# Layer 0's residual by a second, block-transposed load of x, and an SP queue that issues each transfer as soon as its buffer is free

## The chip, the core and the metric

The kernel runs on one core of one Trainium2 chip. The metric is device microseconds of one execution of the whole program. The core has TensorE (PE) for matmuls, VectorE (DVE), ScalarE (ACT), GpSimd (POOL) and SyncE (SP), which here only issues DMA transfers. Each engine runs its own list of instructions in order. They wait for each other through semaphores alone, written out by hand.

## The reference

The input x has 64 images of 256 x 256 pixels with 16 channels, in float32. Two layers follow each other, and each adds a convolution of the normalised input to the input:

```python
def _gn(v, G=8, eps=1e-5):      # mean and variance over height, width and the 2 channels of a group
    ...
    return ((g - m) / jnp.sqrt(s + eps)).reshape(v.shape)
kern = jnp.einsum('lj,lk,li->ijkl', u, w, v)          # 3 x 3 kernel, 16 channels to 16, of rank one per output channel
out  = lax.conv_general_dilated(inputs, kern, window_strides=(1, 1), padding='SAME', ...)
x = x + relu(conv(_gn(x)) + b)     # layer 0, with u, v, w, b of L0
x = x + relu(conv(_gn(x)) + b)     # layer 1, with those of L1
```

## The kernel before, in words

**Layout.** One image at a time stays in SBUF. A DMA brings rows of x into `raw` (two rows of the image to a partition, `a` being the row of the two), and DVE transposes 32 x 32 blocks into `evens` (`N0`): a partition then holds a channel and a column parity within a quarter of the height, and the free dimension holds pairs of columns and 64 rows. Layer 0 writes its sum into `odds` (`T1`, two buffers, by image): there a quadrant of 32 partitions holds a quarter of the width, with all 256 rows, and the pairs of columns are shifted by one column. Layer 1 reads `odds` and ends in `result` (`T2`), which DVE transposes into `pixels` for the store.

**Rounds.** Each layer of each image has four rounds (`f` = 0 to 3) of 8 column pairs. A round of a layer is, on PE, 6 taps of the convolution (6 x 16 matmuls of 32 x 32 weights over 512 columns) into `ps_y`, and 2 more such groups (32 matmuls, with the constant 0/1 weights `perm`) into `ps_x`: these move the layer's input, the residual, into the layout of the output. ACT makes relu(`ps_y` + bias) into `R` (`relu`, L454 for layer 0 and L457 for layer 1), and DVE adds `ps_x` and `R` (`add`, L574 and L571). `ps_y` and `ps_x` fill the whole of PSUM, so there is one of each: the convolution of the next round waits for `relued`, the next residual product for `added`.

**Order.** The program's loop over `p` runs layer 0 of image `p` (4 rounds), then layer 1 of image `p - 1` (4 rounds). In layer 0, DVE follows each add by `turn_in` of image `p + 1` (L554). In layer 1 it follows each add by `turn_out` (L586). The sums for the normalisations are built beside this: of squares by ACT (L430), of `evens` by POOL (`folds`, L280), of the layer 0 result by the accumulator of the relu (`partial_relu`) plus the sum of x (L605, L606). Small matmuls (`group_sums` L299, `bias_product` L309) stand in the middle of certain rounds, after their third tap (`HOOK_AFTER`); they write into `ps_x` and wait there for `added`, and the following residual product waits for `mini_read`, i.e. until DVE has read their result (L612, L635). `wrap_pair` (L319) adds 16 small matmuls to round 0 of layer 0.

**Transfers.** All are issued by SP into one queue: per image 8 loads of `raw` (L186) and 8 stores of `pixels` (L196), 448 to 576 KB each. The function `pass_on` paces them: a load waits for the residual product of the round before (`x_filled`), a store for the convolution of the round (`y_filled`), so that one is issued about every half round.

Of the kernel before, what the change touches and what calls it, by code (L numbers as in the profile page):

```python
# [7 lines left out]
IMAGES, H, W, C = 64, 256, 256, 16  # L8
P = 128
Q = 32  # L10
# [24 lines left out]
TURNS = HALVES * ROUNDS + 4  # L35
HALO0, HALO1 = 2 * (QUADS - 1), QUADS
ODDS_SUM, ODDS_PAD = 1, 2
EVENS_SUM = 2
HOOK_AFTER = 2

# [38 lines left out]

def norms_before(y, p):  # L80
    return 2 * p + y


def squares_at(kind, p):

    if kind == "odds":
        return ROUNDS * (2 * p + 2) + (ROUNDS - 1 if p + 1 < IMAGES else 0)
    return ROUNDS * (2 * p + 1)


def build(nc, x, params, consts, out):
# [7 lines left out]

    with ExitStack() as ctx:  # L100
        def sb(name, shape):
            return ctx.enter_context(nc.sbuf_tensor(name, shape, fp32))
# [8 lines left out]
        pixels = sb("pixels", [P, HALVES, ROW])  # L111
# [13 lines left out]
        acc_relu = sb("partial_relu", [P, ROUNDS])  # L125
        sums = [sb(f"sums{y}", [P, 2]) for y in range(2)]
        mom = [sb(f"moments{y}", [P, 2]) for y in range(2)]
        center = [mom[y][:, 0:1] for y in range(2)]
# [3 lines left out]
        bias = sb("bias", [P, 2])  # L132
# [35 lines left out]
        turned_out = sem("turned_out")  # L168

# [3 lines left out]
        def _(sp):  # L173
# [15 lines left out]
            def store(p, f, a):  # L189
# [3 lines left out]
                if ROUNDS * p + f:  # L193
# [3 lines left out]
                             pixels[:, a, :].rearrange("p (q y) -> p q y", q=QUADS)[:, :, part]  # L197
                             ).then_inc(image_out[a], 16)

            def pass_on(n, loaded, stored):  # L200
                if n:
                    sp.wait_ge(x_filled, n)
                load(*loaded)
                sp.wait_ge(y_filled, n + 1)
                store(*stored)

            for p in range(2):
                for f in range(ROUNDS):
                    for a in range(HALVES):
                        if p == 0 or f < ROUNDS - 1 or a == 0:  # L210
                            load(p, f, a)
            for p in range(IMAGES + 1):
                if p < IMAGES:
                    pass_on(round_of(0, p, 0), (p + 1, 3, 1), (p - 2, 1, 1))
                    pass_on(round_of(0, p, 1), (p + 2, 0, 0), (p - 2, 2, 0))
                    pass_on(round_of(0, p, 2), (p + 2, 0, 1), (p - 2, 2, 1))
                    pass_on(round_of(0, p, 3), (p + 2, 1, 0), (p - 2, 3, 0))
                else:
                    store(p - 2, 1, 1)
                    store(p - 2, 2, 0)  # L220
                    store(p - 2, 2, 1)
                    store(p - 2, 3, 0)
                if p:
                    pass_on(round_of(1, p - 1, 0), (p + 2, 1, 1), (p - 2, 3, 1))
                    pass_on(round_of(1, p - 1, 1), (p + 2, 2, 0), (p - 1, 0, 0))
                    pass_on(round_of(1, p - 1, 2), (p + 2, 2, 1), (p - 1, 0, 1))
                    pass_on(round_of(1, p - 1, 3), (p + 2, 3, 0), (p - 1, 1, 0))
                else:
                    load(p + 2, 1, 1)
                    load(p + 2, 2, 0)  # L230
                    load(p + 2, 2, 1)
                    load(p + 2, 3, 0)
            store(IMAGES - 1, 1, 1)
            for f in (2, 3):
                for a in range(HALVES):
                    store(IMAGES - 1, f, a)
# [54 lines left out]
        def _(pe):  # L291
# [30 lines left out]
            def conv0(p, f):  # L322
                n = round_of(0, p, f)
                if n:
                    pe.wait_ge(relued, n)
                if f == 0:
                    pe.wait_ge(scaled0, p + 1)
                    pe.wait_ge(padded0, p + 1)
                    pe.wait_ge(halo0, HALO0 * (p + 1))
                for t in range(NTAP):  # L330
                    side, i = t // TAPS, t % TAPS
                    for q in range(QUADS):
                        for r in range(QUADS):
                            k = SLOTS * q + EACH * f + side
                            rows, part = slice(Q * r, Q * (r + 1)), slice(Q * q, Q * (q + 1))
                            done = nc.tensor.matmul(ps_y[part, r, :], w0[rows, t * Q:(t + 1) * Q],  # L336
# [9 lines left out]
                if n:  # L346
                    pe.wait_ge(added, n)
                if f == 0:
                    pe.wait_ge(mini_read, MINI["bias", 0, p] + 1)
                for side in range(SIDES):  # L350
                    for q in range(QUADS):
                        for r in range(QUADS):
                            k = SLOTS * q + EACH * f + side
                            done = nc.tensor.matmul(ps_x[Q * q:Q * (q + 1), r, :], perm[Q * r:Q * (r + 1), side, :],  # L354
                                                    N0[Q * r:Q * (r + 1), k:k + EACH, 1:1 + HQ],
                                                    start=(side == 0), stop=(side == SIDES - 1))
                done.then_inc(x_filled, 1)

            def conv1(p, f):
                n = round_of(1, p, f)  # L360
                t1 = T1[p % 2]
                pe.wait_ge(relued, n)
# [57 lines left out]
        def _(act):  # L420
# [11 lines left out]

            def stats_of_evens(p, f):
# [6 lines left out]
            def stats_of_odds(p, f):  # L440
                act.wait_ge(added, round_of(0, p, f) + 1)
                square(T1[p % 2][:, EACH * f:EACH * (f + 1), 1:1 + H],
                       junk[:].rearrange("p q x -> p (q x)")[:, 0:EACH * H].rearrange("p (k h) -> p k h", h=H),
                       acc[1][:, f:f + 1])

            def relu(y, p, f):
                n = round_of(y, p, f)
# [270 lines left out]
```

## Time and profile before

| | us |
|---|---|
| median of 3 runs | 4696.13 (4691.48 to 4697.93) |
| profiled execution | 4676.86 |
| its span in the trace | 4675.1 |
| PE busy | 4587.9 (98%) |
| DVE busy | 2845.1 (61%) |
| ACT busy | 2199.5 (47%) |
| POOL busy | 1265.0 (27%) |
| DMA queue of SP, share of 16 engines | 35.0% |

The granted TensorE clock is 0.997 of full speed over the span. The trace's PE records have ends that are modelled and overlap, so "98% busy" says that PE is hardly ever empty, not that no time is lost between rounds; the starts of the instructions tell more. The work repeats itself image by image: the layer 0 convolution of one image starts at 2331.06 us, and that of the image 31 later at 4559.63 us.

### The profile page before, as it was taken

The numbers are of one execution on the slowest core, as the hardware profiler recorded it, in microseconds if no ns is written. First come the engines' busy times: TensorE is split into PE (matmuls) and PEld (weight loads), VectorE is DVE, ScalarE is ACT, GpSimd is POOL, SyncE is SP. The second block draws the span as 40 slices with busy tenths as digits, with TensorE's granted clock in tenths as the row PEclk, the third lists the DMA queues.
The fourth block names the chain that finished last, engine by engine and source line by source line (L and its number), as shares of the span: only waits on it lengthen the run. The fifth ranks groups of instructions, "written<-read, shape, count | busy, mean of one in ns | idle before, by whom it ended". The sixth has DMA issues, their size and how long they took to land.

```text
span 4675.1 us, 288889 instructions
## 1 busy us (share of the span) xinstructions
PE 4587.9 (98%) x138240; PEld 2626.0 (56%) x138240; DVE 2845.1 (61%) x3341; ACT 2199.5 (47%) x2242; POOL 1265.0 (27%) x1093
## 2 busy tenths in 40 slices
PE   5999999999999999999999999999999999999999
PEld 3555555555555555555555555555555555555555
DVE  4656656566566566665666656656656666566564
ACT  4454444544445444444454444444544444445442
POOL 3322322323223222232232322322313223223230
PEclk9999999999999999999999999999999999999999
DMA  3333333333333333333333333333333333333323
GB/s 120 108 120 117 124 121 122 118 122 116 122 121 120 118 119 120 123 118 121 122 119 121 121 120 121 120 121 122 120 121 121 120 125 117 121 122 120 121 91 102
DMA packets 542278, 555.71 MB, mean 119 GB/s; under 512 B 16432, under 2 KB 541104, under 8 KB 541104
## 3 DMA queue, kind: packets, MB, share of 16 engines
q1 hardware_dynamic: 541104, 537.22, 35.0%
q8 instruction: 1083, 17.74, 1.6%
q14 instruction: 91, 0.75, 0.1%
HBM read 268.72 MB, written 268.44 MB: 115 GB/s over the span
## 4 chain that ended last, share of the span: by engine, by line
PE 94%; issue 3%; ACT 1%; DVE 0%; ACTq 0%; DVEq 0%
PE ps_y L374 35%; PE ps_y L336 34%; PE ps_x L399 12%; PE ps_x L354 10%; PE ps_y L319 2%; PE ps_x L299 1%; ACT relu L457 1%; ACT relu L454 0%; PE ps_x L309 0%; DVE evens L554 0%; DVE result L571 0%; ACTq L452 0%; DVE pixels L586 0%; DVEq L100 0%; ACT evens L465 0%
## 5 line engine op out<-in xcount | busy, mean ns | idle before, releaser
L374 PE MATMUL ps_y<-odds,scaled 32*32 32x512 f32 x49152 | 1766.8, 600 | 7.9 <-issue 2.2
L336 PE MATMUL ps_y<-evens,scaled 32*32 32x512 f32 x49152 | 1745.3, 598 | 23.6 <-ACT evens L465 8.3
L574 DVE TENSOR_TENSOR odds<-ps_x,relu 128x2048 f32<-128x2048 f32 x256 | 586.8, 2292 | 1110.7 <-PE ps_x L354 842.1
L374 PEld LDWEIGHTS ps_y<-odds,scaled 32*32 32x32 f32 x49152 | 808.0, 103 | 794.2 <-issue 376.4
L336 PEld LDWEIGHTS ps_y<-evens,scaled 32*32 32x32 f32 x49152 | 852.8, 103 | 699.8 <-issue 214.0
L457 ACT ACTIVATE relu<-ps_y,bias 128x2048 f32<-128x2048 f32 x256 | 503.8, 1968 | 1094.3 <-PE ps_y L374 942.7
L280 POOL TENSOR_TENSOR fold<-fold,evens 128x1024 f32<-128x1024 f32 x384 | 845.0, 2200 | 597.3 <-DVE evens L561 309.8
L571 DVE TENSOR_TENSOR result<-ps_x,relu 128x2048 f32<-128x2048 f32 x256 | 586.6, 2292 | 636.4 <-PE ps_x L399 439.2
L454 ACT ACTIVATE relu<-ps_y,bias 128x2048 f32<-128x2048 f32 x256 | 503.7, 1968 | 920.8 <-PE ps_y L336 910.6
L354 PE MATMUL ps_x<-evens,constants 32*32 32x512 f32 x16384 | 786.7, 596 | 0.0
L399 PE MATMUL ps_x<-odds,constants 32*32 32x512 f32 x16384 | 776.2, 604 | 0.0
L267 POOL COPY odds<-odds 32x256 f32<-32x256 f32 x256 | 102.0, 399 | 2078.3 <-DVE odds L574 2066.5
L554 DVE STREAM_TRANSPOSE evens<-raw 128x1024 f32<-128x1024 f32 (+2 forms) x512 | 621.6, 1260 | 5.2 <-DMA raw<-in_x 5.2
L430 ACT ACTIVATE junk<-odds 128x2048 f32<-128x2048 f32 x256 | 490.6, 1917 | 282.8 <-DVE odds L574 282.8
L586 DVE STREAM_TRANSPOSE pixels<-result 128x1024 f32<-128x1024 f32 x512 | 618.3, 1251 | 4.5
L354 PEld LDWEIGHTS ps_x<-evens,constants 32*32 32x32 f32 x16384 | 406.8, 103 | 161.7 <-issue 13.9
L399 PEld LDWEIGHTS ps_x<-odds,constants 32*32 32x32 f32 x16384 | 406.3, 103 | 155.9 <-issue 9.7
L430 ACT ACTIVATE junk<-evens 128x2048 f32<-128x2048 f32 (+2 forms) x256 | 487.7, 1905 | 7.3 <-DVE evens L561 4.5
L280 POOL TENSOR_TENSOR fold<-evens 128x1024 f32<-128x1024 f32 x64 | 153.2, 2394 | 603.4 <-DVE evens L554 603.4
L299 PE MATMUL ps_x<-sums,constants 32*32 32x2 f32 x4096 | 122.9, 173 | 45.0 <-DVE sums L602 39.1
L299 PEld LDWEIGHTS ps_x<-sums,constants 32*32 32x32 f32 x4096 | 100.5, 103 | 80.6 <-issue 38.5
L606 DVE TENSOR_TENSOR sums<-sums 128x1 f32<-128x1 f32 x64 | 134.3, 2099 | 2.2
(49 smaller groups left out, 1266.7 us busy)
## 6 DMA issues: line engine op xcount, KB each, us to landing
out<-pixels SPq DMA_DIRECT2D x512, 512.0 KB, 3.5
raw<-in_x SPq DMA_DIRECT2D x256, 512.0 KB, 3.9
raw<-in_x SPq DMA_DIRECT2D x128, 576.0 KB, 4.1
raw<-in_x SPq DMA_DIRECT2D x128, 448.0 KB, 3.5
parameters<-in_params SPq DMA_DIRECT2D x2, 96.5 KB, 2.0
constants<-in_consts SPq DMA_DIRECT2D x1, 81.0 KB, 2.0
```

What stands on the lines that cost most here:

```text
L280: nc.gpsimd.tensor_tensor(to, chunk(0) if d == 1 else to, chunk(d), ALU.add).then_inc(folded, 1)
L336: done = nc.tensor.matmul(ps_y[part, r, :], w0[rows, t * Q:(t + 1) * Q], N0[rows, k:k + EACH, i:i + HQ], start=(t == 0), stop=(t == NTAP - ...
L354: done = nc.tensor.matmul(ps_x[Q * q:Q * (q + 1), r, :], perm[Q * r:Q * (r + 1), side, :], N0[Q * r:Q * (r + 1), k:k + EACH, 1:1 + HQ], st ...
L374: done = nc.tensor.matmul(ps_y[Q * r:Q * (r + 1), q, :], w1[p % 2][Q * q:Q * (q + 1), t * Q:(t + 1) * Q], t1[Q * q:Q * (q + 1), k:k + EACH ...
L399: done = nc.tensor.matmul(ps_x[Q * r:Q * (r + 1), q, :], perm[Q * q:Q * (q + 1), side, :], t1[Q * q:Q * (q + 1), k:k + EACH, 1 + HQ * r:1 ...
L430: nc.scalar.activation(into, source, ACT.Square, accum_out=to).then_inc(squared, 1)
L454: ins = nc.scalar.activation(R[:], ps_y[:], ACT.Relu, bias=bias[:, 0:1], accum_out=acc_relu[:, f:f + 1])
L457: ins = nc.scalar.activation(R[:], ps_y[:], ACT.Relu, bias=bias[:, 1:2])
L554: nc.vector.transpose(turned[:, a, 1:1 + PAIRS, :].rearrange("p (q k) g -> p q k g", q=QUADS)[:, :, freed(f), :], pixels_in[:, :, freed(f) ...
L571: nc.vector.tensor_tensor(T2[:].rearrange("p q k h -> p q (k h)"), ps_x[:], R[:], ALU.add).then_inc(added, 1)
L574: nc.vector.tensor_tensor(T1[p % 2][:, EACH * f:EACH * (f + 1), 1:1 + H].rearrange("p k (r h) -> p r k h", h=HQ), ps_x[:].rearrange("p r ( ...
L586: nc.vector.transpose(to[:, :, EACH * f:EACH * (f + 1), :], result[:, a, :, :].rearrange("p (q k) g -> p q k g", q=QUADS)).then_inc(turned ...
```

## The change

What PE, ACT and DVE do for layer 0 is divided anew; layer 1 stays nearly as it was.

- PE: the residual product of layer 0 (32 matmuls a round, L354) is gone. The convolution's rounds use `ps_y` and `ps_x` in turn, and wait for the `added` of two rounds back. Round 1 waits for `mini_read` of the bias, since it writes `ps_x`.
- The residual comes from x by a second load. `load_rest` fetches, for each round, 1 MB in four DMAs of 32 partitions x 8 x 256 elements (for round 0, 240 elements, and four more DMAs of 32 x 8 x 16 for the column before) into `rest`, a ring of two rounds. DVE's `turn_rest` transposes it into `odds` in two halves of 128 x 1024 a round, spread by the tables `REST_IN_0` (within layer 0) and `REST_IN_1` (for the next image, within layer 1).
- `rectify_and_add` takes the place of ACT's relu and DVE's add in layer 0: four instructions of 128 x 512 a round compute max(`ps`, -bias) + `odds` in place. The result lacks the bias, a constant per channel, which is put back where `odds` is used: as a scalar in layer 1's `add`, and in the statistics (`center_odds`, and ACT's two passes over the round, `Square` and `Identity`, both with the bias, in place of relu plus one `Square`).
- SP: no `pass_on`. Loads, rest loads and stores stand in one fixed order, and each waits only for its buffer (and for the transfer before it of its own kind). `pixels` becomes a ring of two rounds of its own.

The diff, cut to what the prediction speaks of:

```diff
+RES_DMAS = (2 * QUADS, QUADS, QUADS, QUADS)
+REST_IN_0 = ((2, 1), (3, 0), (3, 1))
+REST_IN_1 = (((0, 0), (0, 1)), (), ((1, 0),), ((1, 1), (2, 0)))
@@ SP
+            def load_rest(p, f):
+                ...
+                    sp.wait_ge(rest_turned, HALVES * (ROUNDS * p + f - RING + 1))
+                size = EACH * Q
+                for q in range(QUADS):
+                    part, to = slice(Q * q, Q * (q + 1)), rest[Q * q:Q * (q + 1), f % RING, :, :]
+                    start = size * f - C
+                    if start >= 0:
+                        sp.dma_start(to, x_quarters[p, q][:, :, start:start + size]).then_inc(rest_in[f % RING], 16)
+                ...
-                    pass_on(round_of(0, p, 0), (p + 1, 3, 1), (p - 2, 1, 1))
-                    pass_on(round_of(0, p, 1), (p + 2, 0, 0), (p - 2, 2, 0))
+                    load(p + 1, 3, 1)
+                    load_rest(p, 3)
+                    store_both(p - 2, 3)
+                    load(p + 2, 0, 0)
+                    load_rest(p + 1, 0)
+                    load(p + 2, 0, 1)
+                    load(p + 2, 1, 0)
+                    load_rest(p + 1, 1)
+                ...
@@ PE conv0
-                if n:
-                    pe.wait_ge(relued, n)
+                ps = (ps_y, ps_x)[f % 2]
+                if f == 1:
+                    pe.wait_ge(mini_read, MINI["bias", 0, p] + 1)
+                if n > 1:
+                    pe.wait_ge(added, n - 1)
                 ...
-                for side in range(SIDES):
-                    for q in range(QUADS):
-                        for r in range(QUADS):
-                            k = SLOTS * q + EACH * f + side
-                            done = nc.tensor.matmul(ps_x[Q * q:Q * (q + 1), r, :], perm[Q * r:Q * (r + 1), side, :],
-                ...
@@ ACT
+                shifted(chunk, into, ACT.Square, bias[p % 2][:], acc[1][:, f:f + 1])
+                shifted(chunk, into, ACT.Identity, bias[p % 2][:], acc_odds[:, f:f + 1])
@@ DVE
+            def turn_rest(p, f, half):
+                ...
+                dve.wait_ge(rest_in[f % RING], 16 * rest_in_by(p, f))
+                if p > 1:
+                    dve.wait_ge(x_filled, relus_before(p - 2, f) + 1)
+                ...
+                nc.vector.transpose(T1[p % 2][:, k:k + each, 1:1 + H].rearrange("p k (j h) -> p j k h", h=Q),
+                                    source.rearrange("p j (k x) -> p j k x", x=Q)).then_inc(rest_turned, 1)
+            def rectify_and_add(p, f):
+                ...
+                dve.wait_ge(rest_turned, HALVES * (ROUNDS * p + f + 1))
+                ...
+                dve.wait_ge(y_filled, n + 1)
+                for r in range(QUADS):
+                    odds = T1[p % 2][:, EACH * f:EACH * (f + 1), 1 + HQ * r:1 + HQ * (r + 1)]
+                    done = nc.vector.scalar_tensor_tensor(odds, ps[:, r, :].rearrange("p (k h) -> p k h", h=HQ),
+                                                          floor[p % 2][:], odds, ALU.max, ALU.add)
+                done.then_inc(added, 1)
@@ DVE, main loop
-                        add(0, p, f)
+                        rectify_and_add(p, f)
+                        if f < ROUNDS - 1:
+                            turn_rest(p, *REST_IN_0[f])
                         if p + 1 < IMAGES:
                             turn_in(p + 1, f)
```

On PE, at layer 0 of one image in the middle of the program (rounds 1 to 3, then the start of layer 1), there stood:

```order
L336 MATMUL ps_y<-evens,scaled 32x512 x96
L354 MATMUL ps_x<-evens,constants 32x512 x32
L336 MATMUL ps_y<-evens,scaled 32x512 x96
L354 MATMUL ps_x<-evens,constants 32x512 x32
L336 MATMUL ps_y<-evens,scaled 32x512 x96
L354 MATMUL ps_x<-evens,constants 32x512 x32
L374 MATMUL ps_y<-odds,scaled 32x512 x48
L309 MATMUL ps_x<-moments,scaled 32x1 x4
```

and now, at the same place (L383 is layer 0's convolution, L412 layer 1's, L351 the bias product):

```order
L383 MATMUL ps_x<-evens,scaled 32x512 x96
L383 MATMUL ps_y<-evens,scaled 32x512 x96
L383 MATMUL ps_x<-evens,scaled 32x512 x96
L412 MATMUL ps_y<-odds,scaled 32x512 x48
L351 MATMUL ps_x<-center_odds,scaled 32x1 x4
```

The convolutions of layer 0 now follow each other directly, in the two halves of PSUM by turns.

On DVE, from the start of layer 0 of an image, there stood (L574 the add, L551 and L554 the transposes of the next image):

```order
L574 TENSOR_TENSOR odds<-ps_x,relu 128x4x8x64
L551 COPY ends<-raw 128x2x16
L554 STREAM_TRANSPOSE evens<-raw 128x4x7x32 x2
L574 TENSOR_TENSOR odds<-ps_x,relu 128x4x8x64
L554 STREAM_TRANSPOSE evens<-raw 128x4x8x32 x2
```

and now, from the last round of layer 1 on (L631 layer 1's add, L641 `turn_out`, L610 `turn_rest`, L695 and L696 the bias and its negative, L622 `rectify_and_add`, L591 `turn_in`):

```order
L631 SCALAR_TENSOR_TENSOR result<-ps_x,bias,relu 128x2048
L641 STREAM_TRANSPOSE pixels<-result 128x1024 x2
L610 STREAM_TRANSPOSE odds<-rest 128x8x4x32 x2
L695 TENSOR_TENSOR bias<-parameters,ps_x 128x1
L696 TENSOR_SCALAR floor<-bias 128x1
L622 SCALAR_TENSOR_TENSOR odds<-ps_y,floor,odds 128x8x64 x4
L610 STREAM_TRANSPOSE odds<-rest 128x8x4x32
L588 COPY ends<-raw 128x2x16
L591 STREAM_TRANSPOSE evens<-raw 128x4x7x32 x2
L622 SCALAR_TENSOR_TENSOR odds<-ps_x,floor,odds 128x8x64 x4
L610 STREAM_TRANSPOSE odds<-rest 128x8x4x32
L591 STREAM_TRANSPOSE evens<-raw 128x4x8x32 x2
```

Two rest transposes stand between the last `turn_out` and the reading of the bias, and one between `rectify_and_add` and `turn_in` in each of rounds 0 to 2; `rectify_and_add` is four instructions where the add was one.

## Rows read from the trace of the kernel before

**Rows 1.** The page's busy time: engine, busy us, share of span, instructions.

```profile
PE 4587.9 (98%) x138240; PEld 2626.0 (56%) x138240; DVE 2845.1 (61%) x3341; ACT 2199.5 (47%) x2242; POOL 1265.0 (27%) x1093
```

**Rows 2.** Chain that ended last, two rounds: start us, us, what.

```profile
2340.35 6.15 PE ps_y L336 x166
...
2346.93 2.11 PE ps_x L354 x57
2349.05 0.04 issue
2349.08 6.15 PE ps_y L336 x167
...
2357.81 6.15 PE ps_y L336 x166
...
2366.53 3.24 PE ps_y L374 x69
```

**Rows 3.** Timeline of such a round: start us, us, engine, line, [idle before <-releaser].

```profile
2346.97 1.97 ACT L454 ACTIVATE relu<-ps_y,bias 128x2048 f32<-128x2048 f32 x1 [2.25 <-PE ps_y L336]
2349.08 0.24 PEld L336 LDWEIGHTS ps_y<-evens,scaled 32*32 32x32 f32 x32 [0.94 <-ACT relu L454]
2357.88 2.29 DVE L574 TENSOR_TENSOR odds<-ps_x,relu 128x2048 f32<-128x2048 f32 x1 [4.06 <-PE ps_x L354]
2360.09 2.43 DVE L554 STREAM_TRANSPOSE evens<-raw 128x1024 f32<-128x1024 f32 x2
```

**Rows 4.** Timeline, PE at the first layer 0 matmuls of two images.

```profile
2331.06 1.16 PE L336 MATMUL ps_y<-evens,scaled 32*32 32x512 f32 x32
...
4559.63 0.70 PE L336 MATMUL ps_y<-evens,scaled 32*32 32x512 f32 x16
```

**Rows 5.** Groups by line and form: busy us, mean ns of one, idle before.

```profile
L574 DVE TENSOR_TENSOR odds<-ps_x,relu 128x2048 f32<-128x2048 f32 x256 | 586.8, 2292 | 1110.7 <-PE ps_x L354 842.1 <-ACT relu L454 268.6
L554 DVE STREAM_TRANSPOSE evens<-raw 128x1024 f32<-128x1024 f32 x256 | 311.6, 1263 | 3.2 <-DMA raw<-in_x 3.2
L554 DVE STREAM_TRANSPOSE evens<-raw 128x1152 f32<-128x1152 f32 x128 | 171.9, 1388 | 2.0 <-DMA raw<-in_x 2.0
L554 DVE STREAM_TRANSPOSE evens<-raw 128x896 f32<-128x896 f32 x128 | 138.1, 1126 | 0.0
L606 DVE TENSOR_TENSOR sums<-sums 128x1 f32<-128x1 f32 x64 | 134.3, 2099 | 2.2
L616 DVE TENSOR_SCALAR small<-moments,small 128x1 f32<-128x1 f32 x128 | 27.4, 214 | 4.6
L625 DVE TENSOR_SCALAR small<-small 128x1 f32<-128x1 f32 x128 | 19.7, 154 | 4.3
L280 POOL TENSOR_TENSOR fold<-fold,evens 128x1024 f32<-128x1024 f32 x384 | 845.0, 2200 | 597.3 <-DVE evens L561 309.8 <-DVE evens L554 250.8
L430 ACT ACTIVATE junk<-odds 128x2048 f32<-128x2048 f32 x256 | 490.6, 1917 | 282.8 <-DVE odds L574 282.8
L430 ACT ACTIVATION_READ_ACCUMULATOR junk<-odds 128x1 f32 x256 | 47.5, 186 | 0.0
```

**Rows 6.** Busy time in one image's stretch: PE, PEld, DVE, ACT, POOL, clock, DMA.

```profile
2300.00:2371.50 71.50, 71.31 (x2174) 40.70 (x2159) 44.26 (x51) 34.31 (x35) 19.78 (x17) 1.00 0.37 121
```

**Rows 7.** DMA queues: packets, MB, share of 16 engines; then issues to landing.

```profile
q1 hardware_dynamic: 541104, 537.22, 35.0%
q8 instruction: 1083, 17.74, 1.6%
...
out<-pixels SPq DMA_DIRECT2D x512, 512.0 KB, 3.5
raw<-in_x SPq DMA_DIRECT2D x256, 512.0 KB, 3.9
```

**Rows 8.** Timeline, PE's weight loads in layer 1 after a `group_sums`.

```profile
2318.06 0.72 PEld L374 LDWEIGHTS ps_y<-odds,scaled 32*32 32x32 f32 x33 [0.75 <-issue]
```

More of the change, by code:

```diff
@@ L77, with relus_before, rest_in_by @@
 MINI = small_products()
+def relus_before(p, f):
+    return ROUNDS * p + f
+def rest_in_by(p, f):
+    both = (RES_DMAS[f % RING], RES_DMAS[f % RING + RING])
+    return sum(both) * p + sum(both[:f // RING + 1])
 def norms_before(y, p):
@@ L131, in build @@
         edge = sb("edge", [P, 1])
-        bias = sb("bias", [P, 2])
+        bias = [sb(f"bias{i}", [P, 1]) for i in range(2)]
+        floor = [sb(f"floor{i}", [P, 1]) for i in range(2)]
+        bias1 = sb("bias_result", [P, 1])
         ps_y = ctx.enter_context(nc.psum_tensor("ps_y", [P, QUADS, BANK], fp32))
@@ L168, in build @@
         turned_out = sem("turned_out")
+        rest_in = [sem(f"rest_in{i}") for i in range(RING)]
+        rest_turned = sem("rest_turned")
         block = ctx.enter_context(nc.Block())
@@ L212, in _, with store_both @@
+            def store_both(p, f):
+                for a in range(HALVES):
+                    store(p, f, a)
+            for f in range(ROUNDS):
+                for a in range(HALVES):
+                    load(0, f, a)
+            load_rest(0, 0)
+            load_rest(0, 1)
+            for f in range(ROUNDS):
+                for a in range(HALVES):
+                    if f < ROUNDS - 1 or a == 0:
+                        load(1, f, a)
+            load_rest(0, 2)
             for p in range(IMAGES + 1):
@@ L223, in _ @@
[L223 to L232, printed above, removed]
@@ L237, in _ @@
+                n = round_of(1, p - 1, 0) if p else 0
+                load(p + 2, 1, 1)
+                for f in range(1, ROUNDS):
+                    load(p + 2, *((2, 0), (2, 1), (3, 0))[f - 1])
+                    if p:
+                        store_both(p - 1, f - 1)
+                    if f == 1:
+                        load_rest(p + 1, 2)
+            store_both(IMAGES - 1, 3)
             for a in range(HALVES):
@@ L335, in conv0 @@
                             rows, part = slice(Q * r, Q * (r + 1)), slice(Q * q, Q * (q + 1))
-                            done = nc.tensor.matmul(ps_y[part, r, :], w0[rows, t * Q:(t + 1) * Q],
+                            done = nc.tensor.matmul(ps[part, r, :], w0[rows, t * Q:(t + 1) * Q],
                                                     N0[rows, k:k + EACH, i:i + HQ], start=(t == 0),
@@ L431, in square, with shifted @@
                 squares[0] += 1
+            def shifted(source, into, function, by, to):
+                act.wait_ge(squared, squares[0])
+                nc.scalar.activation(into, source, function, bias=by, accum_out=to).then_inc(squared, 1)
+                squares[0] += 1
             def stats_of_evens(p, f):
@@ new lines, in rectify_and_add @@
+            def rectify_and_add(p, f):
+                n = round_of(0, p, f)
+                ps = (ps_y, ps_x)[f % 2]
+                dve.wait_ge(rest_turned, HALVES * (ROUNDS * p + f + 1))
+                if f == 0:
+                    dve.wait_ge(mini_read, MINI["bias", 0, p] + 1)
+                dve.wait_ge(y_filled, n + 1)
[4 more added lines that the diff above has]
+                done.then_inc(added, 1)
@@ L634, in take_bias @@
                 dve.wait_ge(mini_filled, MINI["bias", y, p] + 1)
[L635 to L636 removed]
+                given, product = par[y][:, PRM - 1:PRM], ps_x[:, 0, 0:1]
+                if y:
+                    nc.vector.tensor_tensor(bias1[:], given, product, ALU.subtract).then_inc(mini_read, 1)
+                else:
+                    step(nc.vector.tensor_tensor(bias[p % 2][:], given, product, ALU.subtract))
+                    nc.vector.tensor_scalar(floor[p % 2][:], bias[p % 2][:], -1.0, None, ALU.mult).then_inc(mini_read, 1)
             dve.wait_ge(const_in, 16 * 3)
@@ L645, in _ @@
             scale_weights(0, 0)
+            for f, half in ((0, 0), (0, 1), (1, 0), (1, 1), (2, 0)):
+                turn_rest(0, f, half)
             for p in range(IMAGES + 1):
```

143 lines of the change are left out of this document (65 added, 78 removed).

## The prediction

> **What bounds the kernel now.** I read the page's busy times first: PE is busy 98% of the span, DVE 61%, ACT 47% [rows 1]. The chain of waits then shows what a round of layer 0 consists of: the convolution starts at 2340.35, its results are complete at 2346.93, the residual product's last part takes 2.11 us more, and the next convolution starts at 2349.08, then at 2357.81 and, with layer 1, at 2366.53 [rows 2]. A round is thus 8.73 us. The timeline of the same round shows a second condition which falls at the same moment: ACT's relu starts at 2346.97 and takes 1.97 us, and PE's next weights have waited 0.94 us for it [rows 3]. So 2.15 us of each layer 0 round lie behind the convolution's end, covered by two things at once, the residual product and the relu that frees `ps_y`. To win them both must go, and the change does both: no product, and the other half of PSUM for the next round. DVE is not in this chain: it idles 1110.7 us before its adds [rows 5]. From the first layer 0 matmul of one image to that of the image 31 later are 4559.63 - 2331.06 = 2228.57 us [rows 4], 71.89 us an image; 64 of these are 4601 us, and the start and the end take the other 74.
>
> **What is removed on PE.** A round has 128 matmuls of one size; 96 stay. By count a round becomes 8.73 x 96/128 = 6.55 us; by the chain, 8.73 - 2.11 - 0.04 = 6.58. The true step may be a little under this, since the 8.73 still holds the idle turn to the next convolution. I take 6.5 (at least 6.4). Saved: 2.23 us a round, 8.9 an image with the same in round 0, whose small matmuls stay. Layer 1's rounds keep their chain: one `ps_y`, relu by ACT, product into `ps_x`.
>
> **DVE, the engine that gets the work.** Two neighbours in a row give what one instruction adds: the add starts at 2357.88 and lasts 2.29, and the transposes behind it start at 2360.09, so instructions overlap by 0.08 us [rows 3].
> - Rest transposes: 8 an image of 128 x 1024. The same form into `evens` takes 1.263 us [rows 5], 1.18 with the overlap: + 9.4 us an image. Source and target strides differ, which no row shows; between 1.1 and 1.6 us each, I take 1.26.
> - `rectify_and_add`: the add of 2048 elements takes 2.292 us. The transposes of 896 and 1152 elements take 1126 and 1388 ns, 1.02 ns an element [rows 5]; at that slope the add has 2.10 us for its elements and 0.19 once per instruction. A quarter of the elements gives 0.52 + 0.19 = 0.72 us. A scalar read from a tile costs more: 214 ns with two such against 154 with none [rows 5], 0.03 each. I take 0.75; the bounds are 0.57 (a quarter of 2.292, nothing once per instruction) and 2 x 0.72 (the two operations taken in turn). Four are 0.75 + 3 x 0.67 = 2.76 us for 2.29: + 0.5 a round, 1.9 an image.
> - Gone: L606, 2.1 us an image, and L605. L606 is one element per partition and takes 2099 ns, as much as POOL's fold of 2200 ns [rows 5]: with both its inputs in SBUF it waits until the fold is over. The new `center_odds` step is of that kind too; it stands where the folds should have ended, so I count 0.2 us, and know it can be 2.3.
>
> The Trainium skill (VectorE: DVE Perf Modes, The TRN2 errata) says that the fixed latency falls between instructions, so one large tile pays it once and many small tiles pay it per tile, and gives (N + 151)/0.96 ns for an fp32 add. The trace agrees for N = 2048 (2291 against 2292). By it a quarter takes 0.69 us and four of them 2.52 with the overlap, 0.2 more than the one add: it speaks against the split, by less than my own term.
>
> DVE's load becomes 44.3 [rows 6] + 9.4 + 1.9 + 1.2 (layer 1's add now reads a scalar as well, bias and floor) - 2.2 = 54.6 us in some 64. In layer 0 alone it is tighter: a middle round is 2.68 (rectify, to the next start) + 1.18 (rest) + 2.35 (turn_in) = 6.2 us against PE's 6.5. ACT there has two passes over `odds`, each 1.92 + 0.19 less 0.1, and one over `evens`: about 6.1. Three engines are within 6% of each other in layer 0, but each has room, and PSUM holds two rounds, so PE goes on.
>
> **Waits that take the place.** I follow an image from the end of round 3 of layer 0 (call it 0).
> 1. DVE's last rectify ends at 2.8; PE's bias product, after three taps of layer 1, comes at 3.25 and needs it: no wait, 0.45 us to spare. `turn_in` of round 3 (3.2 us) ends at 5.9, then the bias is read; PE wants it at 6.5. No wait.
> 2. ACT's two passes over round 3 run from 2.8 to 6.9; the relu of layer 1, whose matmuls are done at 6.6, runs 6.9 to 8.9. PE's product is over at 8.65: waits 0.3.
> 3. DVE: add from 8.9, `turn_out`, two rest transposes, free at 8.9 + 2.27 + 2.35 + 2.36 = 15.9; only then does it read the group sums which PE's product of round 1 (at 15.7) waits for: 0.35.
> 4. Round 3 of layer 1: from its convolution's end, relu and product 2.2, then 2.27 + 2.35 + 2.36 and bias and floor 0.4 on DVE: 9.6. PE has meanwhile 2.15 of product and 7.1 of layer 0's round 0 and stands before round 1, which now needs `mini_read`: 9.25. Waits 0.35 to 0.6.
>
> Together 1.1 us; with as much again for things that shift, I take 1.4 (0 to 3).
>
> **Transfers.** Now 16 an image; the change adds 4 MB in 16 DMAs of 256 KB and the four short ones of 64-byte pieces. The queue has 35.0% of 16 engines for 537.22 MB [rows 7], i.e. 48.4 ns for a packet of about 1 KB, 25.2 us an image. Another 4096 such packets give 12.4 us, the 1024 short ones at most 3.1: 41 us in 64, with q8 some 66%. The nearest deadline: the rest load of round 3 is issued when (1, 1) has been turned, just before layer 0 starts its round 1, and is needed one and a half rounds after, 10 us later; alone it takes about 5 (two landings of 512 KB at 3.5 to 3.9 [rows 7] overlap). Behind it in SP's order stand two stores whose buffer is needed four rounds on. All other transfers have 15 us or more. SP is blocked for long stretches at waits for `rest_turned`, but what stands behind is due later. So I price the transfers at nothing, with DMA as cover for DVE's transposes; the removal of the pacing is worth nothing either way as long as 66% leaves the gaps. The Trainium skill (SBUF — State Buffer, Door 1: The DMA port swizzle) says that 32 partitions reach 8 of 16 ports, 189 GB/s against 328 at 1 MiB. By it the rest's packets would cost 1.7 times as much, about 50 us of DMA in 64, still under the period; no transfer before covers 32 partitions, so no row here shows it.
>
> **The sum.** Per image -8.9 + 1.4 = -7.5 us, x 64 = -480. The first image waits some 3 us more for its rest loads. From the profiled execution's 4676.9: 4200. The median of the runs is 0.4% above that execution, 4696.1 against 4676.9, so as a median 4217; the turn-around of 0.1 us a round that I left in 6.5 pulls down, 4210.
>
> **Rivals.**
> - *DVE becomes the bound in layer 0.* If a rectify instruction takes 0.95 instead of 0.75, DVE's round is 7.0 us against 6.5. It loses 1.5 us over three rounds, 0.8 at the last, less the 0.45 spare at the bias product: 1.8 an image, 115 us, 4325. The same from rest transposes of 1.5 us. For it: the form is in no row, and the room is 0.3 us a round. Against: the add of the same traffic runs at one element a cycle. At twice 0.72 a round is 8.8 us, as now, and with the waits the time about 4,700.
> - *PE starves for instructions.* After `group_sums` PE's weights have waited 0.75 us with no releaser [rows 8]; instructions come over the same DMA engines (q8 [rows 7]). With bursts of rest loads in front of them, two more such pauses with their follow-up (1.1 each) an image give 2.2 x 64 = 140: 4350. Against: q8 takes 1.6% and PE has fewer instructions per image than before.
> - *The rest loads bound the kernel: slower.* If their packets (32-partition pieces of 1 KB, starting 64 bytes off) take long, the queue is full. It decides against the kernel when 25.2 + 1.2 + 4096 packets / 16 engines x t exceeds 71.9 us: t = 178 ns, 3.7 times a packet of today. At 190 ns: 75 us an image, 64 x 75 + 75 = 4,880. Against: nothing in a packet is different but the place; for: no row shows one.
> - *No change*: PE finds another wait of 2.2 us in each round. The double PSUM excludes it unless DVE is late by a whole round.
>
> **Numbers.** Forecast 0.68, own range 4130 to 4270 (all waits gone and 6.4 a round: -9.1 x 64 = -582, 4113 as a median; three us of waits: 4310). DVE-bound 0.17, starved 0.08, rest-bound 0.05, no change 0.02. The likeliest time is 4210; the range 4130 to 4400 takes in the second and third case. A difference of 0.2% is what runs of this kernel can tell from none. Faster 0.94, same 0.01, slower 0.05.
>
> **What would show it.** Starts of layer 0's convolutions 6.5 us apart; rectify at 0.75 us and rest transposes at 1.26; DVE near 85% busy; waits of PE before layer 0's round 1 and before layer 1's products, none of a microsecond; a DMA share of 60 to 70%, and next to no wait of DVE for `rest`. It would be wrong if DVE waits for DMA in every image, if the clock falls, or if PE's convolutions stand 7 us apart.

## The result: 4.5% slower, not 10% faster

| | before | changed |
|---|---|---|
| median of 4 runs, us | 4693.81 (4680.48 to 4697.93) | 4901.74 (4880.29 to 4924.5) |
| ratio | | 1.0449 (1.0389 to 1.0509) |
| profiled execution, its span, us | 4676.86, 4675.1 | 4916.27, 4914.5 |
| mean granted clock of TensorE | 0.997 | 0.971 |

The forecast was 4210, the range 4130 to 4400. The page of the changed kernel gives busy time, the PE row of its 40 slices with the clock, the queues, the chain's shares by engine, and the DMA issues (KB each, us to landing):

```profile
PE 4273.1 (87%) x121856; PEld 2374.9 (48%) x121856; DVE 3430.3 (70%) x4685; ACT 2253.0 (46%) x2242; POOL 1264.3 (26%) x1093
...
PEclk8999999999999999999999999999999999999999
...
q1 hardware_dynamic: 889264, 805.73, 64.5%
q8 instruction: 955, 15.65, 1.4%
...
PE 69%; issue 16%; DVE 10%; ACT 4%; DMA 1%; SPq 0%; POOL 0%; DVEq 0%; ACTq 0%; POOLq 0%
...
out<-pixels SPq DMA_DIRECT2D x512, 512.0 KB, 4.5
rest<-in_x SPq DMA_DIRECT2D x768, 256.0 KB, 5.3
raw<-in_x SPq DMA_DIRECT2D x256, 512.0 KB, 7.9
```

PE has 12% fewer matmuls than in [rows 1] and is busy for 315 us less, yet the span is 239 us longer: PE stands idle. No engine has taken its place as the bound, for 16% of the chain is "issue", time in which the engine waited for nothing that the profile shows. The list of waits (engine, line, releaser: us in total, times, longest) says the same. Of the changed kernel:

```profile
PEld ps_y L412 <- issue: 588.4, 1046, 4.2
...
PEld ps_y L383 <- issue: 378.6, 428, 4.9
PEld ps_x L383 <- issue: 310.5, 388, 4.4
```

The kernel before has 376.4, 214.0 and 98.7 us in its three largest rows of the kind. What the forecast had feared for DVE is not there. The groups by form:

```profile
L610 DVE STREAM_TRANSPOSE odds<-rest 128x1024 f32<-128x1024 f32 x512 | 615.3, 1225 | 12.8 <-DMA rest<-in_x 12.8
...
L631 DVE SCALAR_TENSOR_TENSOR result<-ps_x,bias,relu 128x2048 f32<-128x2048 f32 x256 | 601.9, 2351 | 838.8 <-PE ps_x L437 482.0 <-ACT relu L496 295.8 <-issue 61.1
L622 DVE SCALAR_TENSOR_TENSOR odds<-ps_x,floor,odds 128x512 f32<-128x512 f32 x512 | 349.0, 746 | 241.2 <-PE ps_x L383 240.9
```

`rectify_and_add` takes 746 ns (forecast 0.75 us), a rest transpose 1225 (1.26), and DVE waits once for `rest`, 12.8 us, 54 us after the start of the program: from then on the data come in time. What comes late is seen in the timeline of layer 0 of one image. First PE's weight loads (start us, us, ..., [idle before]), then what SP issues, then the DMA of 2320 to 2339 (row DMA: busy tenths in 40 slices).

```profile
2326.83 0.24 PEld L383 LDWEIGHTS ps_x<-evens,scaled 32*32 32x32 f32 x32 [2.62 <-issue]
...
2332.22 0.24 PEld L383 LDWEIGHTS ps_y<-evens,scaled 32*32 32x32 f32 x32 [1.83 <-issue]
...
2339.26 0.24 PEld L383 LDWEIGHTS ps_x<-evens,scaled 32*32 32x32 f32 x32 [3.50 <-issue]
```

```profile
2317.84 2.60 SPq L233 DMA_DIRECT2D rest<-in_x  x4
2320.53 0.95 SPq L219 DMA_DIRECT2D out<-pixels  x2
2326.39 0.38 SPq L209 DMA_DIRECT2D raw<-in_x  x1
2326.82 1.98 SPq L235 DMA_DIRECT2D rest<-in_x  x4
2328.84 2.57 SPq L240 DMA_DIRECT2D rest<-in_x  x4
2331.51 4.22 SPq L209 DMA_DIRECT2D raw<-in_x  x2
```

```profile
DMA  8569999999999994869999999999999699856994
...
q1 hardware_dynamic: 5656, 4.34, 98.9%
q8 instruction: 3, 0.05, 1.1%
```

The last of these rows is the key: in 19 us only three packets of the queue "instruction" were moved. They carry 16 KB each (15.65 MB by 955) and are called fetches below. In the kernel before, the same length (2330 to 2349) has five, four of them started in gaps between the transfers:

```profile
DMA  9991202998001000000999400000010002899599
...
q1 hardware_dynamic: 2455, 2.45, 38.5%
q8 instruction: 5, 0.08, 1.9%
```

The records give each packet its time. In the changed kernel fetches run 2324.19 to 2325.35, 2329.55 to 2330.55 and 2336.69 to 2337.78, and PE resumes at 2326.83, 2332.22 and 2339.26: each time 1.5 to 1.7 us after the end of a fetch. The Trainium skill (Runtime: NRT & Kernel Launch, Instruction fetch mechanics) says that an engine's instructions are refilled in blocks of 16 KiB, 256 instructions, over a DMA queue of its own. The counts agree: 955 x 256 = 244,480, and PE has 121,856 matmuls and as many weight loads, 243,712. That the cost is "mostly hidden", as the page has it, holds for the kernel before and not for this one.

### The profile page after: what moved, and what is told of

The parts are those of the page before. It is cut to its first block, busy times and chain, and to the rows that moved or that the text cites. A ratio compares the mean times of both kernels' runs of the same rounds, so it can differ in the third digit from the quotient of the medians.

```text
span 4914.5 us, 258958 instructions
## 1 busy us (share of the span) xinstructions
PE 4273.1 (87%) x121856; PEld 2374.9 (48%) x121856; DVE 3430.3 (70%) x4685; ACT 2253.0 (46%) x2242; POOL 1264.3 (26%) x1093
## 2 busy tenths in 40 slices
DMA packets 890332, 822.31 MB, mean 167 GB/s; under 512 B 102448, under 2 KB 889264, under 8 KB 889264
## 3 DMA queue, kind: packets, MB, share of 16 engines
q1 hardware_dynamic: 889264, 805.73, 64.5%
q8 instruction: 955, 15.65, 1.4%
## 4 chain that ended last, share of the span: by engine, by line
PE 69%; issue 16%; DVE 10%; ACT 4%; DMA 1%; SPq 0%; POOL 0%; DVEq 0%; ACTq 0%; POOLq 0%
PE ps_y L412 25%; PE ps_x L383 17%; PE ps_y L383 15%; PE ps_x L437 9%; DVE result L631 4%; DVE odds L610 4%; ACT relu L496 3%; DVE pixels L641 2%; PE ps_y L361 1%; DMA raw<-in_x 1%; DVE odds L622 1%; PE ps_x L341 1%; ACT junk L473 1%; PE ps_x L351 0%; DVE evens L591 0%
## 5 line engine op out<-in xcount | busy, mean ns | idle before, releaser
L412 PE MATMUL ps_y<-odds,scaled 32*32 32x512 f32 x49152 | 1972.2, 614 | 200.2 <-issue 195.9
L473 ACT ACTIVATE junk<-odds,bias 128x2048 f32<-128x2048 f32 x512 | 1026.7, 2005 | 1140.6 <-DVE odds L622 1131.1
L412 PEld LDWEIGHTS ps_y<-odds,scaled 32*32 32x32 f32 x49152 | 944.6, 104 | 944.1 <-issue 588.4
L631 DVE SCALAR_TENSOR_TENSOR result<-ps_x,bias,relu 128x2048 f32<-128x2048 f32 x256 | 601.9, 2351 | 838.8 <-PE ps_x L437 482.0
L383 PE MATMUL ps_y<-evens,scaled 32*32 32x512 f32 x24576 | 1007.3, 616 | 153.1 <-issue 134.5
L383 PE MATMUL ps_x<-evens,scaled 32*32 32x512 f32 x24576 | 986.7, 623 | 148.5 <-issue 136.3
L496 ACT ACTIVATE relu<-ps_y,bias_result 128x2048 f32<-128x2048 f32 x256 | 503.7, 1968 | 1303.2 <-PE ps_y L412 1179.4
L383 PEld LDWEIGHTS ps_x<-evens,scaled 32*32 32x32 f32 x24576 | 519.2, 105 | 527.1 <-issue 310.5
L383 PEld LDWEIGHTS ps_y<-evens,scaled 32*32 32x32 f32 x24576 | 430.6, 104 | 482.1 <-issue 378.6
L610 DVE STREAM_TRANSPOSE odds<-rest 128x1024 f32<-128x1024 f32 x512 | 615.3, 1225 | 12.8 <-DMA rest<-in_x 12.8
L591 DVE STREAM_TRANSPOSE evens<-raw 128x1024 f32<-128x1024 f32 (+2 forms) x512 | 611.0, 1240 | 7.7 <-DMA raw<-in_x 7.7
L641 DVE STREAM_TRANSPOSE pixels<-result 128x1024 f32<-128x1024 f32 x512 | 612.7, 1239 | 4.5
L622 DVE SCALAR_TENSOR_TENSOR odds<-ps_x,floor,odds 128x512 f32<-128x512 f32 x512 | 349.0, 746 | 241.2 <-PE ps_x L383 240.9
L622 DVE SCALAR_TENSOR_TENSOR odds<-ps_y,floor,odds 128x512 f32<-128x512 f32 x512 | 349.0, 745 | 241.2 <-PE ps_y L383 239.4
```

What stands on the lines that cost most here:

```text
L383: done = nc.tensor.matmul(ps[part, r, :], w0[rows, t * Q:(t + 1) * Q], N0[rows, k:k + EACH, i:i + HQ], start=(t == 0), stop=(t == NTAP - 1 ...
L412: done = nc.tensor.matmul(ps_y[Q * r:Q * (r + 1), q, :], w1[p % 2][Q * q:Q * (q + 1), t * Q:(t + 1) * Q], t1[Q * q:Q * (q + 1), k:k + EACH ...
L473: nc.scalar.activation(into, source, function, bias=by, accum_out=to).then_inc(squared, 1)
L496: nc.scalar.activation(R[:], ps_y[:], ACT.Relu, bias=bias1[:]).then_inc(relued, 1)
L591: nc.vector.transpose(turned[:, a, 1:1 + PAIRS, :].rearrange("p (q k) g -> p q k g", q=QUADS)[:, :, freed(f), :], pixels_in[:, :, freed(f) ...
L610: nc.vector.transpose(T1[p % 2][:, k:k + each, 1:1 + H].rearrange("p k (j h) -> p j k h", h=Q), source.rearrange("p j (k x) -> p j k x", x ...
```

## One count for all runs

A pause is here a space of 0.72 us or more between the starts of two of PE's matmuls; the time at the half clock leaves out the first 150 us of a run. A fetch ends every 5.1 us in the changed kernel, so by chance 0.7 / 5.1 = 14% of the pauses would end 1.1 to 1.8 us after one. "Explained" is the growth of the pauses against the reference run, plus half of the growth in time at the half clock; "measured" is the growth of the span.

| run | pauses: number, us | of them 1.1 to 1.8 us after a fetch, us | at clock 0.5, us | reference | explained | measured |
|---|---|---|---|---|---|---|
| before | 41, 56 | 19 | 9 | | | |
| e2_before_unpaced | 241, 345 | 288 | 28 | before | 299 | 288 |
| g3_before_half | 163, 196 | 136 | 10 | before | 141 | 192 |
| f3_before_runs | 259, 411 | 348 | 45 | before | 373 | 391 |
| f2_before_spread | 325, 461 | 396 | 51 | before | 426 | 476 |
| e4_before_rest | 353, 611 | 545 | 161 | before | 631 | 582 |
| f4_before_act_queue | 341, 758 | 684 | 370 | before | 883 | 804 |
| f0_once_paced | 196, 236 | 96 | 6 | | | |
| e1_rest_once | 272, 315 | 188 | 7 | f0 | 80 | 105 |
| f1_paced | 400, 589 | 479 | 81 | f0 | 391 | 444 |
| e3_window | 478, 780 | 653 | 115 | f0 | 599 | 613 |
| changed kernel | 507, 884 | 696 | 253 | f0 | 772 | 743 |

In every run the pauses and the clock together make up the lost time within 80 us, and in those that lose 190 us or more, 69% to 90% of the pauses' time ends in that window after a fetch. "Half of the growth" is an estimate: it takes a matmul at 1.2 GHz for twice as long as one at 2.4.

The DMA records also show why a fetch comes late. Take as late one that starts over 5.5 us after the fetch before it: 362 of the changed kernel's 955, 45 of 1083 in the kernel before. In the last microsecond before a late fetch starts, the 16 DMA engines of the changed kernel are 101% busy (records overlap a little), before the other fetches 34%. In e2_before_unpaced it is 101% against 16%. Even the 45 late ones of the kernel before stand behind 84%, the others behind 34%.

The clock falls behind some of these pauses. A stretch of layer 1 in the changed kernel, PE's matmuls and then the windows (us, busy time of PE, PEld, DVE, ACT, POOL, clock, DMA):

```profile
2373.64 3.22 PE L412 MATMUL ps_y<-odds,scaled 32*32 32x512 f32 x48 [3.00 <-issue]
```

```profile
2369.00:2374.00 5.00, 2.00 (x80) 1.03 (x87) 3.25 (x8) 0.00 (x0) 0.00 (x0) 0.88 1.04 292
2374.00:2378.00 4.00, 4.00 (x82) 1.99 (x65) 0.00 (x0) 0.25 (x1) 0.00 (x0) 0.50 0.70 214
2378.00:2384.00 6.00, 6.00 (x183) 4.49 (x162) 3.06 (x5) 3.13 (x5) 0.00 (x0) 0.87 0.01 3
```

After these 3.00 us without a matmul the granted clock is 0.50, 1.2 instead of 2.4 GHz, and with it PE is slow for the next microseconds as well. This is the smaller part: by the same estimate 253 us at half speed lose about 127.

## The experiments

Two causes were on the table. The second load of x delays PE's instructions by its 4 MB an image (the expectations' Theory I), or the lost pacing does so, by the bursts in which SP now issues (Theory P). Against both stood that the new DVE and PSUM arrangement itself was slow.

**e1_rest_once: the changed kernel with nearly no rest loads.**

```diff
-                if p >= IMAGES:
+                if p > 0 or f >= RING:
                 ...
-                dve.wait_ge(rest_in[f % RING], 16 * rest_in_by(p, f))
+                dve.wait_ge(rest_in[f % RING], 16 * rest_in_by(0, f % RING))
```

> The changed kernel with the rest load made only for the first two rounds of image 0; DVE transposes the same two slots for every image, so every other image gets a wrong residual in layer 0. All compute instructions stay, 4 MB of 12 MB an image leave the queue; raw loads and stores stay unpaced. Theory I (TensorE starves: its instruction fetches come late behind data bursts in the DMA engines): most of the issue gaps go, 4200 to 4350 us. Theory D (the new chain of DVE, ACT and PSUM waits is what costs): stays at 4850 to 4900, since DVE and ACT do the same. Theory P (missing pacing alone): stays above 4600.

4275.93 us, ratio to before 0.9132 (0.9115 to 0.9150), in the range of Theory I; Theory D and Theory P alone both fall. PE, DVE, ACT and PSUM do all that the change asks of them, and it is 8.7% faster. 626 us of the changed kernel's time hang on bytes which DVE is not late in getting.

**e2_before_unpaced: the kernel before without the two waits of `pass_on`.** Same work, same bytes, same order of transfers.

```diff
-                if n:
-                    sp.wait_ge(x_filled, n)
-                sp.wait_ge(y_filled, n + 1)
```

> The kernel before, with the two pacing waits of pass_on taken out; every load and store goes out when its buffer is free, in the old order. Theory I: the bytes are unchanged, but some transfers now pair up (1 MB at once), so fetches come late now and then: 4700 to 4850. Theory P (pacing is what matters): 4850 or more. Theory D: no change, 4690.

4968.19 us, 1.0612 (1.0594 to 1.0630): what Theory P expected, and above the range of Theory I, which had too small a part for the pacing. Theory D, which expected no change, fails here too. With the queue's share at 34.1% as before, the two removed waits alone cost 6.1%. Rows of it, SP's issues and the weight loads just behind:

```profile
2302.00 0.38 SPq L196 DMA_DIRECT2D out<-pixels  x1
2302.47 0.46 SPq L186 DMA_DIRECT2D raw<-in_x  x1
2303.12 0.91 SPq L196 DMA_DIRECT2D out<-pixels  x1
2332.53 0.37 SPq L186 DMA_DIRECT2D raw<-in_x  x1
```

```profile
2309.64 0.14 PEld L396 LDWEIGHTS ps_x<-odds,constants 32*32 32x32 f32 x6 [2.72 <-issue]
```

Waits for buffers come free together: the issues come in one burst, then nothing for 29 us; and PE pauses behind the burst.

**e3_window: the changed kernel with at most 1 MB in flight.** A `gate` before each transfer waits for the oldest ones to land.

```diff
+            def gate(sem, size, dmas=1, limit=1024):
+                while out and sum(o[2] for o in out) + size > limit:
+                    was, count, _ = out.pop(0)
+                    sp.wait_ge(was, 16 * count)
                 ...
```

> The changed kernel, SP holds at most 1 MB of transfers in flight (a rest quartet alone, or two of 512 KB). Theory I, with the length of the backlog as the cause: shorter backlogs, fewer late fetches, 4500 to 4800; if the total of bytes is the cause rather than the backlog, 4900. Theory D: 4900. If the window makes loads late, DVE shows waits for DMA and the time is above 4900.

4784.43 us, 1.0218 (1.0202 to 1.0234), at the upper end of the 4500 to 4800 expected for the backlog. A shorter queue helps by 117 us and is not enough. The window also makes some loads late: DVE waits for `rest` 30 times, 84.9 us in all, against once in the changed kernel.

**e4_before_rest: the kernel before with the rest loads, unread.** Four DMAs of 256 KB behind every second step of `pass_on`; nothing waits for them but the next four.

```diff
+            def load_rest(p, f):
                 ...
+                if n % 2:
+                    load_rest(loaded[0] % IMAGES, n // 2 % ROUNDS)
```

> The kernel before, with its pacing, plus the rest load's 4 MB an image in groups of four DMAs of 256 KB into a tile that nobody reads. No compute instruction changes. Theory I: TensorE's fetches come late behind the groups of four, 4900 to 5200 us, with issue gaps of 1 to 3 us. Theory D: 4690, extra transfers cost nothing.

5262.61 us, 1.1239 (1.1213 to 1.1265), above what I expected. The old kernel, its pacing kept, loses 583 us to transfers whose data nobody reads. Its two largest rows of "issue" (L389 is layer 1's convolution, L351 layer 0's), where the kernel before has 376.4 and 214.0 us:

```profile
PEld ps_y L389 <- issue: 523.2, 1260, 4.5
...
PEld ps_y L351 <- issue: 358.2, 705, 4.7
```

**f0_once_paced and f1_paced: the transfers of the change in small paced portions.** SP's order is written anew: mostly 256 to 768 KB at a time, each portion behind `y_filled`, `added` or `x_filled` of a round (`at0(1, y_filled, p)` waits for the convolution of round 1 of layer 0 of image `p`). Not every portion came out so small: in f1 four rest DMAs and a store, 1.5 MB, are issued in a row from 2317.30 to 2322.68. f1 makes all the transfers of the change, f0 those of e1 alone.

```diff
                 ...
-                    load(p + 2, 0, 0)
-                    load_rest(p + 1, 0)
-                    load(p + 2, 0, 1)
                 ...
+                at0(1, y_filled, p)
+                load(p + 2, 0, 0)
+                quarter(p + 1, 0, 0)
+                at0(1, added, p)
+                load(p + 2, 0, 1)
+                quarter(p + 1, 0, 1)
                 ...
```

> The changed kernel with its rest load made only for the first two rounds of image 0 (so the residual of layer 0 is wrong for the rest), and raw loads and stores paced: each waits for a fixed point of TensorE's or VectorE's progress, 2 to 4 us apart. Theory I (late instruction fetches behind backlogs of transfers): 4200 to 4240 us, 1% under the unpaced run with one rest load (4276), which would show the forecast's sum for the compute to be right. Theory D (compute waits): no change from 4276.

> The changed kernel with all its transfers, issued in 18 portions an image of 256 to 768 KB at fixed points of progress. Theory I with the backlog as the cause: fewer late fetches than with the 1 MB window (4784), 4400 to 4700. If the sum of bytes is the cause: 4800 to 4900. Theory D: 4900.

f0: 4171.80 us, 0.8897 (0.8884 to 0.8910). f1: 4606.77 us, 0.9827 (0.9799 to 0.9855), again as g5_paced_again 4618.36, 0.9832 (0.9805 to 0.9858). f0 is under the 4200 to 4240 expected, f1 inside its 4400 to 4700. f1 computes all that the kernel before does, and is 1.7% faster than that one: little, but in both runs clear of noise. DVE of f0 in layer 0:

```profile
2350.16 2.73 DVE L666 SCALAR_TENSOR_TENSOR odds<-ps_x,floor,odds 128x512 f32<-128x512 f32 x4
2352.80 1.24 DVE L654 STREAM_TRANSPOSE odds<-rest 128x1024 f32<-128x1024 f32 x1
2353.96 2.39 DVE L635 STREAM_TRANSPOSE evens<-raw 128x1024 f32<-128x1024 f32 x2
2356.24 2.71 DVE L666 SCALAR_TENSOR_TENSOR odds<-ps_y,floor,odds 128x512 f32<-128x512 f32 x4
```

This is the round that the forecast drew, 6.1 us long. The three numbers divide the 730 us between the changed kernel and f0: 4901.74 - 4606.77 = 295 for the missing pacing, 4606.77 - 4171.80 = 435 for the transfers even when paced. The two costs do not simply add: without the rest loads the missing pacing is worth 4275.93 - 4171.80 = 104.

**f2, f3, f4, g3: is it the bursts, the descriptors or the bytes?** All are e4 with another form of the unread loads: f2 spreads them, one DMA of 256 KB behind each load and each store; f3 makes the four DMAs one of 1 MB in runs of 8 KB over 128 partitions; f4 issues them on ScalarE's queue; g3 is f2 with half of them (2 MB an image).

```diff
 f2, in pass_on:
+                quarter()        # behind the load
+                quarter()        # behind the store; g3 has this one alone
 f3:
-                for q in range(QUADS):
-                    sp.dma_start(rest[Q * q:Q * (q + 1)], ...).then_inc(rest_in, 16)
+                sp.dma_start(rest[:], x_runs[p][:, Q * 64 * f:Q * 64 * (f + 1)]).then_inc(rest_in, 16)
 f4, in ACT's program behind every second relu:
+                        nc.scalar.dma_start(rest[Q * q:Q * (q + 1)], x_quarters[...]...).then_inc(rest_in, 16)
```

> The kernel before with the same dummy rest loads as the run with quartets (5262), now one DMA of 256 KB behind each load and each store, so at most 768 KB stand in the queue. Theory I, backlog: 4750 to 5000. If the sum of bytes is the cause: 5260 as before.

> As the run with quartets (5262), but each quartet is one DMA of 1 MB over 128 partitions in runs of 8 KB instead of 1 KB: the same bytes, an eighth of the descriptors. If the fetch waits behind the number of queued descriptors: 4700 to 4900. If behind bytes: 5200 to 5300. Theory D: 4690.

> As the kernel before with dummy rest loads in quartets on SP's queue (5262), but the quartets are issued by ScalarE on its own queue, once every second round. If the fetch waits only behind what stands in the same queue's order, a second queue shares the engines more fairly: 4700 to 4950. If it waits for the DMA engines whatever queue fills them: 5150 to 5350.

> As the kernel before with one dummy DMA of 256 KB behind each load and each store (5148), but only behind each store: 2 MB an image instead of 4. If the loss goes with the bytes: half of 460, 4900 to 4930. If it comes from backlogs over some length: well under that, 4700 to 4850.

| | us | ratio to before |
|---|---|---|
| e4, groups of four | 5262.61 | 1.1239 (1.1213 to 1.1265) |
| f2, spread | 5147.81 | 1.0978 (1.0946 to 1.1010) |
| f3, runs of 8 KB | 5058.78 | 1.0787 (1.0769 to 1.0805) |
| f4, second queue | 5495.16 | 1.1736 (1.1701 to 1.1770) |
| g3, spread, half the bytes | 4863.34 | 1.0376 (1.0354 to 1.0398) |

Spreading gives back 115 us of 583; f2 lies between its two expectations. Half the bytes cost 179 us where all cost 460, somewhat less than half and again between the two expectations; two amounts don't tell a threshold from a curve. Runs of 8 KB help by a third of the loss and leave the rest, which fits neither "descriptors" nor "bytes". But f3 changes two things at once, the length of the runs and the partitions written (128 instead of 32), so which of them helps isn't shown. A second queue is worse, above both expectations, which speaks against a cause in SP's own queue. In f4 ACT's program changes too, since it issues the loads; but PE's weight loads wait 375 us for the relu there, against 461 in the kernel before, so the loss doesn't come that way. The queue rows of f4 allow a price: 0.211 x 5479.2 x 16 / 278,528 = 66 ns for a packet into 32 partitions, against 48.4 in [rows 7]. The same sum for q1, the raw loads and stores of the same run, gives 54 ns (0.331 x 5479.2 x 16 / 541,104).

```profile
q1 hardware_dynamic: 541104, 537.22, 33.1%
q10 hardware_dynamic: 278528, 268.50, 21.1%
```

So these packets take 1.37 times those of [rows 7], and 1.24 times the others of their own run, which share its load. The Trainium skill (SBUF — State Buffer, Door 1: The DMA port swizzle) has 189 GB/s for 32 partitions against 328 for 128, a ratio of 1.7, for transfers of 1 MiB. No run here has such transfers alone, so the two aren't measured alike.

**g4_paced_halves: f1 with the quarters in the order 0, 2, 1, 3.**

```diff
+                q = (0, 2, 1, 3)[q]
```

> The paced version of the changed kernel (4607), with the four rest DMAs of a round in the order of quarters 0, 2, 1, 3, so that two neighbours in the queue write to different halves of the partitions. The Trainium skill (SBUF — State Buffer, Door 1: The DMA port swizzle) says that partitions 0 to 63 share one half of the ports, and that two transfers to different halves hardly gain over one. If the order matters, packets come back from 57 ns towards 50, and the time to 4550; by the page's second sentence it stays at 4600.

4606.47 us, 0.9819 (0.9803 to 0.9835), beside g5_paced_again, which ran f1 itself with it (0.9832, 0.9805 to 0.9858):

> The paced version again, beside the one with the other order: 4590 to 4620, against 4680 before.

The order of the partitions makes no difference that can be told.

## Why the prediction was wrong

- *What bounds the kernel, what is removed on PE*: right in kind. Without the load, paced, the new arrangement takes 4171.80 us (f0), where 4210 was forecast for all of it. The size was off: layer 0's last rounds follow each other in 6.1 us, under the 6.5 taken and even the bound of 6.4. The 6.15 us of the convolution's own row in [rows 2] had it. From its first matmul to layer 1's, layer 0 takes 26.0 us an image in f0 and 36.0 before, 9.9 less, where 8.9 was forecast. (The range's lower end has 9.1 for rounds of 6.4, where four of them save 9.3.)
- *DVE*: right. 746 ns, 1225 ns, 82% busy in f0 (3430.0 of 4171.4; forecast 85%). The DVE-bound rival falls with it. One reading behind the 0.75 was wrong: the instruction of 214 ns (L616) has one scalar from a tile and one number, so such a scalar costs 0.06 us, not 0.03. Layer 1's add says the same (2351 ns with one, 2292 without).
- *Waits in place*: larger than forecast, inside the bounds of 0 to 3. Layer 1 takes 38.2 us an image in f0 and 36.1 before, 2.1 more, where 1.4 was forecast. This and the extra microsecond won in layer 0 nearly cancel: 7.8 us an image are won, forecast 7.5. That f0 ends only 38 us under 4210 is thus in part luck.
- *Transfers, the load itself*: 64.5% and 1.4% of the engines' time, 66% as forecast, but over a span 17% longer: 0.645 x 4914.5 / 64 = 49.5 us an image, where I had 41. A packet of that queue took 57.0 ns on average (0.645 x 4914.5 x 16 / 889,264), not 48.4. `rest` is late once. The rest-bound rival named the right sign and nearly the time (4,880) by a mechanism that is not there: past the start DVE does not wait for `rest`, and packets take 57 ns on average in the changed kernel and 66 into 32 partitions in f4, not 178. That its time came near is chance.
- **The step that failed**: "So I price the transfers at nothing, ... the removal of the pacing is worth nothing either way as long as 66% leaves the gaps." I asked who waits for the data, and no one does. I had the right mechanism among the rivals ("PE starves for instructions") and gave it 140 us, "two more such pauses ... an image", and a chance of 0.08. Measured against f0 it is 648 us of pauses (884 - 236) and 124 of clock, 507 pauses in 64 images, eight an image of 1.7 us. My argument against it was that q8 takes 1.6%: a busy share, where what matters is how late a fetch starts. In [rows 7] stood the number that should have warned me: 1083 fetches in 4675 us, one every 4.3 us. In the changed kernel a quarter of them start within 3.8 us of the one before, and one in twenty within 3.4, which leaves little room between what PE uses and the fastest that was seen. The fetches themselves take 1.07 to 1.21 us on average in every run; it is their starts that slip, 362 of 955 against 45 of 1083. The pacing, whose function I took for unneeded order, left gaps behind the transfers.

What stays open: no run changed PE's stream of instructions or the fetch's own path. That fetches are held up by data packets on the shared DMA engines rests on the coincidence in time (79% of the pauses' time where chance gives 14%), on the engines being full before late fetches and not before the others (101% against 34%), and on six kernels (e2, e4, f2, f3, f4, g3) in which only transfers differ from the kernel before (and, in f4, the engine that issues them). How the DMA engines choose between the two queues isn't shown. Why runs of 8 KB lie between the two theories, and which part of the 435 us of f1 a finer pacing could still win, wasn't tried.

## What to carry to other kernels

A kernel of many small matmuls also lives on a stream of instructions, and DMA engines deliver it: divide the span by the packets of PE's instruction queue, and where that is near the shortest spacing in the trace, count every added megabyte and every burst as PE time, even if no engine waits for the data. Look for "issue" pauses ahead of PE's weight loads before any large transfer is added, and keep the transfers in portions of a few hundred KB behind the compute's own events. Moving PE work to the DMA is worth it only by that account: here it saved some 520 us and cost 730, or 435 when paced.

## What the runs showed of the hardware

- In the last microsecond before a late fetch (over 5.5 us after the one before) the 16 DMA engines are 101% busy in the changed kernel, before the others 34%.
- PE resumes 1.45 us (median; quartiles 1.35 and 1.58) after the end of an instruction fetch, for the 408 pauses of 0.9 us or more in the changed kernel.
- Two waits taken from SP, nothing else, cost 6.1% (e2).
- 4 MB an image whose data no engine reads cost 12.4% at a queue share of 60.2% (e4), and 17.4% from ScalarE's queue at 54.2% in sum (f4): the share of busy time does not rank them.
- Behind a pause of 3.00 us the granted clock was 0.50; past the first 150 us it was so for 253 us in the changed kernel and 370 in f4.
